# Cross attention: the first two batches stacked from SBUF to SBUF by two queues, sums that wait per four heads, products one slot sooner

## The reference, cut to what matters

```
qp = q @ Wq.T;  kv = latent_kv @ Wkv_expand.T;  k, v = split(kv)      # 16 heads of 32 columns
scores = einsum('bhqd,bhkd->bhqk', qh, kh) / sqrt(32)
scores = where(causal, scores, finfo.min);  attn = softmax(scores)
out = einsum('bhqk,bhkd->bhqd', attn, vh).reshape(b, sq, H) @ Wout.T
```

## Time and profile before

| | us |
|---|---|
| median of 3 runs (1181.51 to 1188.59) | 1184.79 |
| profiled execution | 1183.95 |
| its span in the trace | 1182.3 |
| PE busy in it | 1076.5 (91%) |
| DVE, ACT, POOL busy | 683.3, 457.1, 284.0 |

### The profile page before, as it was taken

How to read it: one execution, slowest core, us unless ns; L and a number is a source line. 1 busy time by engine, 2 the same in 40 slices (tenths; PEclk the granted TensorE clock), 3 DMA queues, 4 the chain that set the end, 5 groups by cost and what they waited for, 6 DMA issues and landing times. The chain is left out here.

```text
span 1182.3 us, 19299 instructions
## 1 busy us (share of the span) xinstructions
PE 1076.5 (91%) x6850; PEld 910.4 (77%) x6850; DVE 683.3 (58%) x1517; ACT 457.1 (39%) x808; POOL 284.0 (24%) x370
## 2 busy tenths in 40 slices
PE   5999999998758999998868879999999999899996
PEld 4688888887547877886647669899999989777784
DVE  3746375562535666675344747777777767344475
ACT  4613334143324444453334235555555555221210
POOL 4510101006112232333234121111222110223030
PEclk9999999999968999998979889999999999899999
DMA  4402020303878778874243256766666775523141
GB/s 154 167 1 107 0 106 0 106 0 136 236 176 224 189 209 226 216 194 113 73 156 129 78 162 230 248 224 229 224 236 241 227 238 168 178 72 125 53 147 66
DMA packets 88818, 179.31 MB, mean 152 GB/s; under 512 B 8032, under 2 KB 33632, under 8 KB 87104
## 3 DMA queue, kind: packets, MB, share of 16 engines
q1 hardware_dynamic: 82096, 155.06, 42.1%
q0 software_dynamic: 6672, 23.60, 5.9%
HBM read 136.95 MB, written 41.42 MB: 151 GB/s over the span
## 5 line engine op out<-in xcount | busy, mean ns | idle before, releaser
L45 PE MATMUL e_ps_h<-e_x_lo,e_gu_hi 128*128 128x256 f32 (+1 forms) x552 | 155.9, 282 | 5.0 <-DVE e_x_lo L1812 5.0
L46 PE MATMUL e_ps_h<-e_x_hi,e_gu_lo 128*128 128x256 f32 (+1 forms) x552 | 153.8, 279 | 0.0
L47 PE MATMUL e_ps_h<-e_x_hi,e_gu_hi 128*128 128x256 f32 (+1 forms) x552 | 153.6, 278 | 0.0
L804 DVE CUSTOM_DVE_ANT_0 b_dump<-b_ps_s,b_mask 128x128 f32<-128x128 f32 (+1 forms) x256 | 80.1, 354 | 68.6 <-PE b_ps_s L990 67.4
L45 PE MATMUL a_ps_proj<-a_x_lo,arena 128*128 128x512 f32 x256 | 102.4, 400 | 14.9 <-DVE a_x_lo L295 12.1
L45 PEld LDWEIGHTS e_ps_h<-e_x_lo,e_gu_hi 128*128 128x128 f32 (+1 forms) x552 | 99.4, 180 | 6.3 <-DVE e_gu_lo L1816 5.2
L46 PE MATMUL a_ps_proj<-a_x_hi,arena 128*128 128x512 f32 x256 | 101.9, 398 | 0.0
L47 PE MATMUL a_ps_proj<-a_x_hi,arena 128*128 128x512 f32 x256 | 101.8, 398 | 0.0
L309 DVE SCALAR_TENSOR_TENSOR a_xc<-a_ps_proj,a_taps,a_xc 128x510 f32<-128x510 f32 (+2 forms) x96 | 71.6, 746 | 51.2 <-ACT a_xc L268 49.0
L46 PEld LDWEIGHTS e_ps_h<-e_x_hi,e_gu_lo 128*128 128x128 f32 (+1 forms) x552 | 99.5, 180 | 0.9
L47 PEld LDWEIGHTS e_ps_h<-e_x_hi,e_gu_hi 128*128 128x128 f32 (+1 forms) x552 | 99.4, 180 | 0.0
(11 more groups left out here) (306 smaller groups left out, 2699.7 us busy)
## 6 DMA issues: line engine op xcount, KB each, us to landing
f_gate_up_raw<-we_gate_up SPq DMA_DIRECT2D x88, 352.0 KB, 4.7
qk_split<-arena SPq DMA_DIRECT2D x32, 512.0 KB, 6.2
b_sk<-qk_split SPq DMA_DIRECT2D x48, 256.0 KB, 4.1
b_sq<-qk_split SPq DMA_DIRECT2D x48, 256.0 KB, 5.7
f_down_raw<-we_down SPq DMA_DIRECT2D x23, 512.0 KB, 6.7
y_slots<-f_y_tile SPq DMA_DIRECT2D x23, 512.0 KB, 2.8
f_x_next<-x SPq DMA_DIRECT2D x6, 1024.0 KB, 5.7
f_down_raw<-we_down SPq DMA_DIRECT2D x23, 192.0 KB, 6.7
```

Of the source, the lines that this page charges most:

```text
L45: pe.matmul(out, a_hi, b_lo, start=first, stop=False)
L46: pe.matmul(out, a_lo, b_hi, start=False, stop=False)
L47: return pe.matmul(out, a_hi, b_hi, start=False, stop=last)
L804: ins = dve.tensor_tensor_reduce(dump[:, n % 2, cols], ps_s[:, n % 2, cols], mask[:, cols], -1.0, 3e38, ALU.add, ALU.min, peak[:, u, k, i: ...
```

## The change

Four edits. First, the halves of batches 0 and 1 are stacked without HBM: `load_direct` issues one transfer of 64 KB for each of the three row groups and each of the four heads of a chunk, from `split` straight to `sk` or `sq`; SP issues the 12 for the keys and ACT the 12 for the queries of a half. `split` may only be written again once these have landed, so ACT's `keys` for batches 1 and 2 wait for `stack_loaded` where they waited for `split_stored`. Second, on ACT the maxima of batch 0 (`peaks(0, 0)`) stand ahead of the four normalisations of turn -1. Third, `attend` waits for 15 of the 16 exponentials at its start and then, per group of four heads, for those heads' cuts. Fourth, `normalize` and `rest` stand one slot sooner.

```
+        def load_direct(engine, into, parts, b, u):
+            for r, s in enumerate(parts):
+                for h in range(HC):
+                    engine.dma_start(into[r * HD:(r + 1) * HD, b % 2, u, h:UH:HC].bitcast(F32),
+                                     split[h * HD:(h + 1) * HD, u, s].bitcast(F32)).then_inc(stack_loaded[u], 16)
...
+            def load_keys(b, u):
+                sp.wait_ge(xkq_lo_done, k_count(b, u))
+                load_direct(sp, sk, (KH, KL, KH), b, u)
...
-                if real(t + 2):
+                if t < 0:
+                    load_keys(t + 2, 0)
+                elif real(t + 2):
                     store_k(t + 2, 0)
                 if t == -1:
                     sp.wait_ge(normed_done, TILES)
                     sp.dma_start(x1_dram[LAST], res[:]).then_inc(normed_stored, 16)
...
-                if real(t + 2):
+                if t < 0:
+                    load_keys(t + 2, 1)
+                elif real(t + 2):
                     store_q(t + 2, 0)
                     load_stack(t + 2, 0)
                     store_k(t + 2, 1)
                 if real(t + 1):
                     load_peaks(t + 1, 0)
...
-                        if t and u == 0 and i in (4, 5):
-                            rest(t - 1, i - 4)
+                        if t and u == 0 and i in (3, 4):
+                            rest(t - 1, i - 3)
...
             def keys(b, u):
                 act.wait_ge(xkq_ready, k_count(b, u))
-                if b:
-                    act.wait_ge(split_stored, 32 * (2 * (b - 1) + u + 1))
+                if 1 <= b <= DIRECT:
+                    act.wait_ge(stack_loaded[u], stack_count(b - 1))
+                elif b > DIRECT:
+                    act.wait_ge(split_stored, stored_count(b - 1, u))
...
+            def load_queries(b, u):
+                act.wait_ge(xkq_lo_done, q_count(b, u))
+                load_direct(act, sq, (QL, QH, QH), b, u)
...
-                    for u in range(2):
-                        for i in range(UH):
-                            fill(t, u, i)
+                    for i in range(UH):
+                        fill(t, 0, i)
+                        if t == -1 and i == 1:
+                            load_queries(0, 1)
+                    fill(t, 1, 0)
+                    load_queries(t + 2, 0)
+                    for i in range(1, UH):
+                        fill(t, 1, i)
                     if t == -1:
+                        peaks(0, 0)
+                        load_queries(1, 1)
                         act.wait_ge(ln_step, TILES + 7)
...
-                        peaks(0, 0)
...
-                        if t and u == 0 and i in (2, 3):
-                            normalize(t - 1, i - 2)
+                        if t and u == 0 and i in (1, 2):
+                            normalize(t - 1, i - 1)
...
             def attend(b):
-                pe.wait_ge(cut_done, HEADS * (b + 1))
+                pe.wait_ge(exp_done, HEADS * (b + 1) - 1)
                 for c in range(DC):
+                    pe.wait_ge(cut_done, HEADS * b + HC * (c + 1))
```

More of the change, by code:

```diff
@@ L477, in cross_attention @@
         FIRST_T, END_T = -2, B + 1
+        DIRECT = 2
         NORMED = B - GB
@@ L516, in o_kept_count, with stack_count, stored_count @@
             return 1 + 3 * b + 2 + u
+        def stack_count(b):
+            return 384 * min(b + 1, DIRECT) + 96 * max(b + 1 - DIRECT, 0)
+        def stored_count(b, u):
+            return 32 * (2 * (b - DIRECT) + u + 1)
         def order(b, u, i):
             return HEADS * b + UH * u + i
+        def load_direct(engine, into, parts, b, u):
[3 more added lines that the diff above has]
+                                     split[h * HD:(h + 1) * HD, u, s].bitcast(F32)).then_inc(stack_loaded[u], 16)
         block = ctx.enter_context(nc.Block())
@@ L526, in store_k @@
                 sp.wait_ge(xkq_lo_done, k_count(b, u))
-                if b:
-                    sp.wait_ge(stack_loaded[u], 96 * b)
+                if b > DIRECT:
+                    sp.wait_ge(stack_loaded[u], stack_count(b - 1))
                 sp.dma_start(split_dram[u, KH:KL + 1].rearrange("s p n -> p s n").bitcast(F32),
@@ L537, in load_stack @@
             def load_stack(b, u):
-                sp.wait_ge(split_stored, 32 * (2 * b + u + 1))
-                if b >= 2:
-                    sp.wait_ge(e_ready, order(b - 2, u, UH - 1) + 1)
+                sp.wait_ge(split_stored, stored_count(b, u))
+                sp.wait_ge(e_ready, order(b - 2, u, UH - 1) + 1)
                 for into, parts in ((sk, (KH, KL, KH)), (sq, (QL, QH, QH))):
@@ L589, in _ @@
                     load_peaks(t + 1, 0)
-                if real(t + 2):
+                if t >= 0 and real(t + 2):
                     store_q(t + 2, 1)
@@ L984, in scores @@
                 if i == 0:
-                    pe.wait_ge(stack_loaded[u], 96 * (b + 1))
+                    pe.wait_ge(stack_loaded[u], stack_count(b))
                 if n >= 2:
```

## The result

| | before | changed |
|---|---|---|
| median of 7 runs, us | 1183.83 (1181.51 to 1189.04) | 1197.00 (1191.89 to 1198.88) |
| profiled execution, us | 1183.95 | 1193.73 |
| its span, us | 1182.3 | 1192.0 |
| mean granted clock of TensorE | 0.963 | 0.954 |

The ratio of the times is 1.0089, with a 95% interval of 1.0061 to 1.0117: slower by 13 us in the medians, 9.8 in the profiled executions. The forecast of 1177 and its range (to 1192) missed it; the rival with a chance of 13%, "ACT's and SP's issues set the start", is what happened.

What follows compares the result with a forecast made beforehand. PE, busy 91% of the span, bounds the kernel, so only its waits can give gains. A start loss of 2.7 less a steady gain of 10.2 makes -7.5 us: 1176.4 profiled, 1177 median, range 1166 to 1192.

Steps and rivals of the forecast that it cites:

- ACT's and SP's issues set the start: Rival, 13%: at 0.735 us a piece, five groups of twelve in one chain lose 19.7 at the start; 1194 us.
- 314.7 + 5 I: Start: time of the first product below the peaks, I being twelve issues; forecast 341.7 against 339.00 before.
- the price of an issue: Start: each direct transfer holds its issuing engine 0.45 us, 5.4 a group of twelve; a loss of 2.7 us.
- a rival: Start: issues cost 0.647 us, from the 612 ns loads; start loses 14.5, time 1189 us; chance 17%.
- an end of the range: Start: 0.735 us a piece, from the 702 ns SBUF to SBUF row; 8.8 a group, a loss of 19.7.
- the sums' 9.0 us: Steady turns: PE's 8 waits for the last cut, 1.1 us each turn, would all go.
- the rests' waits: Steady turns: PE's 13.4 us in 8 waits for POOL would go except 1.2 each in turns 6 and 7 and the last 2.3.
- the second halves: Steady turns: PE, 1.49 us earlier, would wait 0.4 to 0.6 us for rows of maxima; 1.2 taken off for turns 4 and 5.
- the transfer chain: Turn openings: SP's stores, stack and rows start at a fixed time in the turn, so PE's gains don't move them.
- the rival of full gains: Rival, 17%: transfers don't hold turns 2 and 3 nor does the clock fall; steady gain 19.0, time 1168.5 us.
- 1.6 us had been set aside: Turn openings: new waits can drop the clock to 0.50; taking this off 11.8 leaves a steady gain of 10.2.
- The margins read off windows: Turns 2 and 3: from when the queue drains to PE's start, 1.0 and 0.6 us can be saved, not 2.6 each.

Runs made afterwards that it cites:

- experiment 5: Changed kernel with each pair of 64 KB direct transfers made one of 128 KB, six a group, scores not the reference's; 1179.09 us, ratio 0.9951 to the kernel before.
- experiment 9: Changed kernel with each group's same bytes in eight one-piece transfers over 96 partitions, scores not the reference's; one run, 1180.37 us.
- experiment 3: Changed kernel with SP issuing batch 0's rows of maxima ahead of the store and the last group of keys; 1181.51 us, ratio 0.9966 to the kernel before.
- experiment 10: Changed kernel with POOL issuing the queries' direct transfers, SP's rows of maxima ahead of store and stack loads; 1168.26 us, ratio 0.9825 to the kernel before.
- Experiment 4: Kernel before with sums per four heads, products one slot sooner, and SP's next-turn rows of maxima ahead of the stack load; 1173.17 us, ratio 0.9886.
- Experiment 1: Kernel before with only the sums per four heads and the products one slot sooner, stacking still by HBM; 1177.67 us, ratio 0.9929.

## Why the prediction was wrong, step by step

**The chain and its formula held.** The first product was put at 314.7 + 5 I. The five groups took 9.53 + 7.74 + 8.29 + 7.72 + 8.43 = 41.7 us, which gives 356.4; measured 356.15. Link by link it holds too: the stretches between the groups and behind the last were 2.6, 3.8, 4.2, 3.4 and 2.95 us, forecast 2.7, 3.6, 4.7, 3.2 and 2.8. With short groups it is too low, since PE's work is no longer hidden behind ACT's issues: by 4.5 us in experiment 5, where ACT's wait for a landing adds to it, and by 2.4 in experiment 9. One call moved on SP (experiment 3) brings the first product 18.1 us forward, which shows that the rows' place behind ACT's last group, the normalisations, the store and SP's keys is what the start waited for. What ACT's groups cost besides shows in experiment 3's wait for the exponential, and goes in experiment 10.

**The step that failed is the price of an issue.** The prediction said: "The new transfer has two pieces on 32 partitions, so it is nearest to the first two: I take 0.45 us a piece, 5.4 a group." A group took 7.7 to 9.5, 0.64 to 0.79 a piece with gaps and a few long ones of up to 2.0 us; the median was 0.618 on ACT. That term, 5 x 5.4 = 27.0, should have been 41.7, and the 14.7 between them is the whole miss of the start (2.7 forecast, 17.15 measured). It was not the transfers that held the issues back: while ACT alone issued its fourth group (334 to 341 us), the DMA engines were busy for a share of 0.38. The row was chosen by the number of pieces. The two rows that share something else with the new transfer, 32 partitions (612 ns) or both ends in SBUF (702 ns), were taken as a rival and as an end of the range, and both were nearer. With three likenesses to choose from and two of them at 0.6 or more, the likeliest value was there, and the slower rival, which decides from 0.67 a piece with gaps, should have had more than 13%. That rival named the mechanism; that its 1194 lies so near the 1193.73 of the profiled execution is in part luck, since it had the start 2.6 us too dear and the steady gain 3.7 too large. Experiments 5 and 9 show that bytes and partitions say little here.

The Trainium skill, "DMA: Bandwidth & Descriptors", section "Issuing engines are not separate DMA queues", has it that a second issuing engine saves only sequencer time, usually small relative to the DMA. The first half agrees as far as rows show: with SP issuing beside ACT (297.5 to 307 us) the DMA share was 0.66, with ACT alone 0.38, which is what more issue time gives while the DMA engines aren't full. The second half does not agree. A landing took 2.0 us and a group's issues 7.7 and more, so here it was the sequencer's time that the kernel waited for.

**The steady part: right in kind, too large in size.** Gone as forecast: the sums' 9.0 us, and the rests' waits in turns 1 to 5. Left: 0.37 and 1.26 in turns 6 and 7, where 1.2 each was forecast, and 2.32 behind the last. New before the second halves: 0.5 each, forecast 0.4 to 0.6. The openings wait for rows in turns 2 to 5 (0.52, 0.63, 1.38, 0.41), where the forecast had turns 3 and 4 alone, so the transfer chain does hold the turns, against the rival of full gains. The steady gain was 6.5, forecast 10.2.

What the forecast had at nothing are the waits of the scores for a stack, 3.7 us in 3 against 0.5 before, one of them (1.11 at 489.53) in turn 3, which took 34.45 us (456.95 to 491.40) against 32.35 before. The clock fell behind two more openings, for which 1.6 us had been set aside. Between the first product and the last `attend` 18.5 us of waits went (9.0 and 9.5) and 9.5 came (rows at openings 3.0, stacks 3.2, second halves 2.5, maxima 0.8), which would leave 9.0. The 2.5 us that are missing fit the clock: as an estimate, twice 3 us with 11.5 matmuls in 2 us where 19.5 are done at 1.00 cost 2.5.

By turns, from one opening to the next: turns 0 to 6 took 36.11, 32.47, 32.22, 34.45, 32.56, 30.25 and 25.74, against 35.04, 33.26, 32.35, 32.35, 32.32, 32.35 and 29.07 before. The margins read off windows let turns 2 and 3 shorten by 1.0 and 0.6; turn 2 shortened by 0.1 and turn 3 grew by 2.1. The gain is in turns 5 to 7 (9.0 us); turns 0 to 4 together lose 2.5.

Experiment 4 shows what SP's order costs in the middle: without the stack load in front of the rows the medians fall by 4.5 us (1177.67 to 1173.17, intervals that overlap), and first product to last `attend` takes 236.1 us in place of 239.6. Experiment 1, which keeps the stacking of before, has a steady gain of 5.5, so the late start didn't spoil it.

**The sum.** 2.7 - 10.2 = -7.5 was forecast; it is 17.15 - 6.5 = +10.6. Of the 18.1 us between them 14.4 are the start and 3.7 the steady turns.

## What to carry to other kernels

Count issues, not bytes: when a transfer is cut in many, number of issues times the price of one is a busy time of the engine that issues them, and it stands in line with that engine's arithmetic. Give them to an engine behind which nobody waits, and put the small transfer that somebody waits for ahead of the long groups. And when no row shows the price of a new operation, list the rows by each likeness (pieces, partitions, ends) and take the one by which most of them agree, not the cheapest that fits.

## What the runs showed of the hardware

- A transfer from SBUF to SBUF issued by ACT or SP held its sequencer for 0.59 to 0.62 us in the median, whether it was 64 KB or 128 KB on 32 partitions or 96 KB on 96; issued by POOL, 0.536 us. It landed 2.0 us after its issue in the median of the changed kernel (64 KB), 2.4 us in experiment 9 (96 KB) and 3.5 in experiment 5 (128 KB).
- ACT's first group was dearer: 9.53 us against 7.7 to 8.3 for the later ones, 5.41 against 3.7 to 4.1 in experiment 5, 5.88 against 5.1 in experiment 9. SP was issuing in the same stretch. ACT's third group, also beside SP, took 8.29 us (8.62 in experiment 3, where the first took 8.51), the second and fourth 7.74 and 7.72. But SP's last group, with ACT silent, took 8.43 all the same, and ACT's third in experiment 9, beside SP, 5.08. Whether the issues of the two engines hinder each other isn't settled by these numbers.
- While PE stood still for 17 us the granted clock was 0.50 (1.2 GHz). After openings with two waits close together (1.50 and 1.35, 1.13 and 0.63, 1.11 and 1.38 us; 0.50 and 1.33 in the kernel before) it fell to that level too, and after those with a single wait of 0.41 and 0.52 it stayed at 1.00.
